# Turning a step's carried-over block behind the step's first head products

## The chip, the cores and the metric

The kernel runs on one core of a Trainium2 chip. The metric is the device time of one execution in microseconds (us), less being better; a change is compared with the kernel before by the median of several runs. Engines work side by side, each through its own instructions in order, and wait for one another by semaphores: PE (TensorE, matrix products), ACT (ScalarE), DVE (VectorE), POOL (GpSimd) and SP (it issues the loads).

## What is computed

Two models run one after the other on 8 sequences of 100 rows of 512 numbers, with a context of 8 x 361 x 512: a single-head cross-attention, then a block with two 16-head cross-attentions and an MLP.

```python
def _cross_attention(q_in, kv_in, wq, bq, wk, bk, wv, bv, wo, bo, bias_k, bias_v):
    qh = (q_in @ wq + bq).reshape(b, q_len, H, K)          # H = 16 heads of K = 128
    kh = concatenate([kv_in @ wk + bk, bias_k])            # 361 + 1 rows
    vh = concatenate([kv_in @ wv + bv, bias_v])
    weights = softmax(einsum('bqhk,bthk->bhqt', qh, kh) / sqrt(K))
    ctx = einsum('bhqt,bthk->bqhk', weights, vh)
    return ctx @ wo + bo

def _forward(x, xf_1, xf_2, ...):
    x = x + _cross_attention(layer_norm(x), xf_1, ...1)
    x = x + _cross_attention(layer_norm(x), xf_2, ...2)
    h = layer_norm(x)
    return x + gelu(h @ w_fc1 + b_fc1) @ w_fc2 + b_fc2
```

## The kernel before

The batch is worked on in two halves of 4 sequences. Each half has two attention layers and the MLP, so there are four **passes** through `layer` (`ph` 0 to 3 in the code, passes 1 to 4 here). Every number is held as two parts, `hi` and `lo`, and every product is three matmuls (`mm3`): hi by hi, lo by hi, hi by lo (lines 608 to 610). So whatever PE leaves in PSUM is first rounded to a `hi` by ACT, and then DVE takes the rest as `lo`; only then can PE read it.

The keys are never formed. A head's query goes through the head's key weights back to the 512 columns of the input ("through keys"), and is scored against the context itself. The 16 heads by 100 rows of a sequence are 1600 rows, cut into 13 blocks of 125 (the last 100). `UNITS` joins the blocks into six units of two blocks (the last of three), and `STEPS` is the list of (unit k, sequence b), 24 steps a pass.

What a step does to a block: **scores** (12 matmuls of 362 columns), the maximum (`maxima` on DVE, a copy and a reduction), the exponential (`exps` on ACT, with a read of the sum), the division (`normalise` on DVE, a reciprocal and a multiplication of `prob`), the **turning** (`turn_probs` on PE, three transposes of `prob` into one PSUM bank, `PT_BANK`), its two parts (`probs_hi` on ACT writes `pT_hi`, `probs_lo` on DVE writes `pT_lo`), and, when both blocks of a unit are turned, `attend` on PE: 36 matmuls of weights by context rows.

The blocks are turned one after the other in their order, and the last block of a step is turned in the next step: the *carried-over* block. `attend` of a step runs in the next step too, and waits for `pt_lo`, which DVE gives with that block's `probs_lo`. Step (2, 3), say, does on PE: scores of its block 0, turning of the block carried over from (2, 2), head products, scores of its block 1, `attend` of (2, 2), turning of its own block 0.

**Head products** fill in between. `PIECES` names, for a place of a step, which products of which head run there: `q` (a head's query, 12 matmuls, one output), `k` (through keys, 12 matmuls, four outputs), `v` (values, 13 matmuls, one output), `o` (projection, 12 matmuls, four outputs, which DVE adds to `xT`). Place "a" lies between the two scores, place "b" at the step's end. Ordinary steps with something in place "a" are, in each pass, these twelve:

- one `k`: (0,1), (0,2), (2,2), (2,3), (4,2), (4,3)
- one `v`: (1,1), (3,1)
- `q` and `o`: (1,2), (3,2)
- `o` and `k`: (1,3), (3,3)

The first two steps of units 2 and 4 (`LATE`) have an order of their own in other branches.

The outputs of head products and of `attend` go round five PSUM banks (`MBUFS`, `free_bank`): an output waits until DVE is through with the one five before it. The weights of head products come by SP through `stage`, and POOL splits them into `wbuf_hi` (line 490) and `wbuf_lo` (line 540), four buffers on; a split waits until PE has used the weights four before. In the first pass there is one thing more: DVE makes ten sums over late key weights (`late_key_sums`, line 1397), each of which waits for a load that is issued behind the sum before.

Every engine runs its list in the order that is written out by hand: for PE, ACT and DVE the loop over `STEPS` at lines 936 to 975, 1265 to 1304 and 1676 to 1725.

Of the kernel before, what the change touches and what calls it, by code (L numbers as in the profile page):

```python
# [68 lines left out]
def pieces(place):  # L69
    return [(word[0], int(word[1:])) for word in PIECES.get(place, "").split()]  # L70
# [61 lines left out]
def build(nc, xT_d, ctxT_d, ctx_d, l0w_d, alpha_d, head_w_d, cols_d, rows_d, norm_d, mlp_w_d, mlp_b_d, out_d):  # L132
# [3 lines left out]
    with ExitStack() as ctx:  # L136
# [468 lines left out]
        def _(pe):  # L605
# [194 lines left out]
            def layer(half, l):  # L800
# [79 lines left out]
                def run_pieces(place, start=0):  # L880
                    for kind, h in pieces(place)[start:]:
                        {"q": queries, "k": through_keys, "v": values, "o": project}[kind](h)

                def scores(k, b, x):
                    i = S_AT[k, b, x]
                    f0, rows = BLOCKS[UNITS[k][x]]
                    last_head = (f0 + rows - 1) // L
                    wait(pe, s_exp, ph * S_LAYER + i - 1)
                    ctx_b = slice(b * T, (b + 1) * T)
                    for c in range(DC):  # L890
                        pe.wait_ge(y_done, ph * R_LAYER + R_AT["k", last_head] + c + 1)
                        mm = mm3(bank[S_BANK + i % 2][0:rows, 0:T], a_hi[:, c, b, ring(f0, rows)],
                                 a_lo[:, c, b, ring(f0, rows)], c_hi[:, c, ctx_b], c_lo[:, c, ctx_b],
                                 start=(c == 0), stop=(c == DC - 1))
                    mm.then_inc(s_mm, 1)
# [38 lines left out]
                before = None  # L934
                for k, b in STEPS:
                    last = None if before is None else (*before, len(UNITS[before[0]]) - 1)
                    if k in LATE and b == 0:
                        scores(k, b, 0)
                        turn_probs(*last)
                        scores(k, b + 1, 0)  # L940
                        attend(*before)
                        turn_probs(k, b, 0)
                        run_pieces((k, b, "b"))
                        scores(k, b, 1)
                    elif k in LATE and b == 1:
                        run_pieces((k, b, "a"))
                        scores(k, b, 1)
                        turn_probs(*last)
                        run_pieces((k, b, "m"))
                        attend(*before)  # L950
                        turn_probs(k, b, 0)
                        run_pieces((k, b, "b"))
                    else:
                        scores(k, b, 0)
                        if before is not None:
                            turn_probs(*last)
                        run_pieces((k, b, "a"))
                        scores(k, b, 1)
                        if before is not None:
                            attend(*before)  # L960
                        turn_probs(k, b, 0)
                        run_pieces((k, b, "b"))
                        if len(UNITS[k]) == 3 and b == 0:
                            turn_probs(k, b, 1)
                            scores(k, b, 2)
                        elif len(UNITS[k]) == 3:
                            scores(k, b, 2)
                            turn_probs(k, b, 1)
                    before = k, b
# [55 lines left out]
        def _(act):  # L1025
# [146 lines left out]
            def layer(half, l):  # L1172
# [44 lines left out]
                def run_pieces(place, start=0):  # L1217
                    for kind, h in pieces(place)[start:]:
                        if kind != "o":
                            {"q": queries_hi, "k": through_keys_hi, "v": values_hi}[kind](h)  # L1220
# [44 lines left out]
                before = None  # L1265
                for k, b in STEPS:
                    last = None if before is None else (*before, len(UNITS[before[0]]) - 1)
                    if k in LATE and b == 0:
                        probs_hi(*last)
                        exps(k, b, 0)  # L1270
                        exps(k, b + 1, 0)
                        first_rows_hi(*before)
                        attended_hi(*before)
                        probs_hi(k, b, 0)
                        run_pieces((k, b, "b"))
                        exps(k, b, 1)
                    elif k in LATE and b == 1:
                        run_pieces((k, b, "a"))
                        probs_hi(*last)
                        run_pieces((k, b, "m"))  # L1280
                        first_rows_hi(*before)
                        attended_hi(*before)
                        probs_hi(k, b, 0)
                        exps(k, b, 1)
                        run_pieces((k, b, "b"))
                    else:
                        if before is not None:
                            probs_hi(*last)
                        exps(k, b, 0)
                        run_pieces((k, b, "a"))  # L1290
                        if before is not None:
                            first_rows_hi(*before)
                        exps(k, b, 1)
                        if before is not None:
                            attended_hi(*before)
                        probs_hi(k, b, 0)
                        run_pieces((k, b, "b"))
                        if len(UNITS[k]) == 3:
                            probs_hi(k, b, 1)
                            exps(k, b, 2)  # L1300
                    before = k, b
# [64 lines left out]
        def _(dve):  # L1366
# [211 lines left out]
            def layer(half, l):  # L1578
# [95 lines left out]
                for k, b in STEPS:  # L1674
                    last = None if before is None else (*before, len(UNITS[before[0]]) - 1)
                    if k in LATE and b == 0:
                        maxima(k, b, 0)
                        probs_lo(*last)
                        normalise(k, b, 0)
                        maxima(k, b + 1, 0)  # L1680
                        normalise(k, b + 1, 0)
                        first_rows_lo(*before)
                        attended_lo(*before)
                        probs_lo(k, b, 0)
                        run_pieces((k, b, "b"))
                        maxima(k, b, 1)
                        normalise(k, b, 1)
                    elif k in LATE and b == 1:
                        run_pieces((k, b, "a"))
                        maxima(k, b, 1)  # L1690
                        probs_lo(*last)
                        run_pieces((k, b, "m"))
                        first_rows_lo(*before)
                        attended_lo(*before)
                        probs_lo(k, b, 0)
                        normalise(k, b, 1)
                        run_pieces((k, b, "b"))
                    else:
                        maxima(k, b, 0)
                        if before is not None:  # L1700
                            probs_lo(*last)
                        normalise(k, b, 0)
                        run_pieces((k, b, "a"))
                        if ph == 0 and "a" in LATE_KEYS_AT.get((k, b), ""):
                            late_key_sums(next(keys))
                        maxima(k, b, 1)
                        if before is not None:
                            first_rows_lo(*before)
                        normalise(k, b, 1)
                        if before is not None:  # L1710
                            attended_lo(*before)
                        probs_lo(k, b, 0)
                        run_pieces((k, b, "b"))
                        if len(UNITS[k]) == 3 and b == 0:
                            probs_lo(k, b, 1)
                            maxima(k, b, 2)
                            normalise(k, b, 2)
                        elif len(UNITS[k]) == 3:
                            maxima(k, b, 2)
                            probs_lo(k, b, 1)  # L1720
                            normalise(k, b, 2)
                    if ph == 0 and "b" in LATE_KEYS_AT.get((k, b), ""):
                        late_key_sums(next(keys))
                    if ph == 0 and (k, b) == (3, 2):
                        key_parts(1)
                    before = k, b
# [114 lines left out]
```

## Time and profile before

| | |
|---|---|
| runs before, median (lowest to highest of 3) | 1829.16 us (1825.69 to 6293.97) |
| profiled execution, device time | 1830.22 us |
| its span (first to last instruction) | 1828.4 us |
| PE busy | 1801.8 us, 99% |
| DVE, ACT, POOL busy | 1125.2, 804.9, 761.4 us |
| mean granted TensorE clock | 0.999 |

The profile is of one execution. A line of the timeline gives start and duration in us from the span's start, the engine, the line of the program, what is written and read, how many instructions are joined, and in brackets how long the engine sat idle before and what ended that.

### The profile page before, as it was taken

How to read it: one execution, taken by the hardware profiler on the slowest of the kernel's cores; microseconds unless marked ns; L12 is line 12 of the kernel's file. 1: busy time of each engine (PE TensorE's matmuls, PEld its weight loads, DVE VectorE, ACT ScalarE, POOL GpSimd, SP SyncE). 2: the span in 40 equal slices, each digit the busy share in tenths (PEclk: the TensorE clock that was granted, in tenths of full speed). 3: DMA queues.
4: the chain of work that ended last, by engine and by line, in shares of the span. 5: the costliest groups of instructions: out<-in, count | busy, mean ns of one | idle time of the engine just before them, and what ended most of it. 6: DMA issues, size and time to landing. Idle time of an engine off the chain costs nothing.

```text
span 1828.4 us, 30720 instructions
## 1 busy us (share of the span) xinstructions
PE 1801.8 (99%) x11524; PEld 1768.3 (97%) x11524; DVE 1125.2 (62%) x2588; ACT 804.9 (44%) x1868; POOL 761.4 (42%) x624
## 2 busy tenths in 40 slices
PE   8989999999999999999999999999999999999999
PEld 5889999999999999999999999999999999999999
DVE  3667656565575565556687655556566556555565
ACT  3634334434344443344475443444435434434354
POOL 2674252352351453531478245252255252352344
PEclk9999999999999999999999999999999999999999
DMA  8833221111120121210373011111022021121132
GB/s 254 241 111 94 62 64 30 47 60 34 33 69 23 41 64 36 59 40 13 127 218 94 30 47 59 35 53 41 24 58 60 24 64 30 47 59 35 46 98 84
DMA packets 73590, 123.80 MB, mean 68 GB/s; under 512 B 13888, under 2 KB 25536, under 8 KB 73444
## 3 DMA queue, kind: packets, MB, share of 16 engines
q1 hardware_dynamic: 71140, 117.64, 22.0%
q10 hardware_dynamic: 2304, 4.20, 0.7%
q8 instruction: 94, 1.54, 0.4%
q14 instruction: 52, 0.43, 0.1%
HBM read 119.20 MB, written 2.61 MB: 67 GB/s over the span
## 4 chain that ended last, share of the span: by engine, by line
PE 88%; DVE 5%; DMA 4%; ACT 1%; SPq 1%; issue 1%; POOL 0%; DVEq 0%; ACTq 0%
PE psum L608 27%; PE psum L609 27%; PE psum L610 27%; PE psum L906 4%; DMA ctxT_in<-ctxT_dram 1%; DMA ctx_rows_in<-ctx_dram 1%; DMA key_stage_late<-head_w_dram 1%; PE psum L779 1%; PE psum L870 1%; PE psum L621 1%; DVE xT L1576 1%; PE psum L617 1%; DVE psum L1544 1%; PE psum L618 0%; PE psum L797 0%
## 5 line engine op out<-in xcount | busy, mean ns | idle before, releaser
L490 POOL TENSOR_TENSOR wbuf_hi<-stage,zero_col 128x512 fp32r<-128x512 f32 x256 | 267.9, 1047 | 917.8 <-PE psum L610 605.1
L540 POOL TENSOR_TENSOR wbuf_lo<-stage,wbuf_hi 128x512 fp32r<-128x512 f32 x256 | 330.2, 1290 | 20.0
L610 PE MATMUL psum<-pT_hi,ctx_rows_lo 121*128 121x250 f32 (+3 forms) x1152 | 332.2, 288 | 0.0
L608 PE MATMUL psum<-pT_hi,ctx_rows_hi 121*128 121x250 f32 (+3 forms) x1152 | 331.6, 288 | 0.0
L609 PE MATMUL psum<-pT_lo,ctx_rows_hi 121*128 121x250 f32 (+3 forms) x1152 | 331.1, 287 | 0.0
L608 PE MATMUL psum<-ctxT_hi,a_hi 128*125 128x362 f32 (+1 forms) x832 | 280.4, 337 | 0.0
L610 PE MATMUL psum<-ctxT_hi,a_lo 128*125 128x362 f32 (+1 forms) x832 | 273.1, 328 | 0.0
L609 PE MATMUL psum<-ctxT_lo,a_hi 128*125 128x362 f32 (+1 forms) x832 | 272.7, 328 | 0.0
L1371 DVE TENSOR_TENSOR a_lo<-psum,a_hi 128x500 fp32r<-128x500 f32 (+2 forms) x288 | 145.9, 526 | 195.1 <-ACT a_hi L1027 194.2
L608 PE MATMUL psum<-a_hi,wbuf_hi 128*128 128x400 f32 x720 | 253.1, 352 | 0.0
L609 PE MATMUL psum<-a_lo,wbuf_hi 128*128 128x400 f32 x720 | 247.8, 344 | 0.0
L610 PE MATMUL psum<-a_hi,wbuf_lo 128*128 128x400 f32 x720 | 247.8, 344 | 0.0
L1027 ACT ACTIVATE a_hi<-psum 128x500 fp32r<-128x500 f32 (+2 forms) x288 | 127.6, 467 | 218.7 <-PE psum L610 217.8
L609 PEld LDWEIGHTS psum<-pT_lo,ctx_rows_hi 121*128 121x128 f32 (+1 forms) x1152 | 219.3, 190 | 0.0
L608 PEld LDWEIGHTS psum<-pT_hi,ctx_rows_hi 121*128 121x128 f32 (+1 forms) x1152 | 218.5, 190 | 0.1
L610 PEld LDWEIGHTS psum<-pT_hi,ctx_rows_lo 121*128 121x128 f32 (+1 forms) x1152 | 217.7, 189 | 0.0
L1231 ACT ACTIVATE prob<-psum,stats 125x362 f32<-125x362 f32 (+1 forms) x208 | 117.3, 564 | 183.1 <-DVE stats L1633 183.1
L1027 ACT ACTIVATE pT_hi<-psum 121x375 fp32r<-121x375 f32 (+1 forms) x208 | 99.9, 480 | 202.8 <-PE psum L906 202.8
L1375 DVE SCALAR_TENSOR_TENSOR a_lo<-psum,cols,a_hi 128x400 fp32r<-128x400 f32 x116 | 73.5, 633 | 175.2 <-ACT a_hi L1214 108.6
L1576 DVE TENSOR_TENSOR xT<-psum,xT 128x400 f32<-128x400 f32 x352 | 176.6, 564 | 0.1
L609 PEld LDWEIGHTS psum<-ctxT_lo,a_hi 128*125 128x125 f32 (+1 forms) x832 | 153.5, 184 | 0.1
L608 PEld LDWEIGHTS psum<-ctxT_hi,a_hi 128*125 128x125 f32 (+1 forms) x832 | 153.3, 184 | 0.1
(185 smaller groups left out, 3549.7 us busy)
## 6 DMA issues: line engine op xcount, KB each, us to landing
stage<-head_w_dram SPq DMA_DIRECT2D x256, 256.0 KB, 2.6
mlp_stage<-mlp_w_dram SPq DMA_DIRECT2D x32, 512.0 KB, 4.2
ctx_rows_in<-ctx_dram SPq DMA_DIRECT2D x12, 726.0 KB
ctxT_in<-ctxT_dram SPq DMA_DIRECT2D x12, 724.0 KB, 11.0
key_stage<-head_w_dram SPq DMA_DIRECT2D x22, 256.0 KB, 8.7
l0w<-l_w_dram ACTq DMA_DIRECT2D x16, 256.0 KB, 9.1
key_stage_late<-head_w_dram SPq DMA_DIRECT2D x10, 256.0 KB, 3.5
out_dram<-y_out SPq DMA_DIRECT2D x8, 200.0 KB, 2.7
```

The costliest lines, as they stand in the source:

```text
L490: return nc.gpsimd.tensor_tensor(out, in_, zero_col[0:in_.shape[0], :].broadcast_to(tuple(in_.shape)), ALU.add)
L540: nc.gpsimd.tensor_tensor(lo, held, hi.bitcast(F32), ALU.subtract).then_inc(stage_free, 1)
L608: pe.matmul(out, a_h, x_hi, start=start, stop=False)
L609: pe.matmul(out, a_h, x_lo, start=False, stop=False)
L610: return pe.matmul(out, a_l, x_hi, start=False, stop=stop)
L617: pe.matmul(out, a_h(c), h_hi[:, c, piece(n)], start=(c == 0), stop=False)
L906: mm = pe.transpose(bank[PT_BANK][0:t_rows, t * PT_STEP:t * PT_STEP + rows], prob[0:rows, i % 2, t0:t0 + t_rows], ident[0:rows, 0:rows])
L1027: return nc.scalar.activation(out, in_, ACT.Copy)
L1231: nc.scalar.activation(prob[0:rows, i % 2, :], bank[S_BANK + i % 2][0:rows, 0:T], ACT.Exp, bias=st[:, 0:1], accum_out=st[:, 2:3]).then_inc ...
L1371: return nc.vector.tensor_tensor(out, value, hi.bitcast(F32), sub)
L1375: return nc.vector.scalar_tensor_tensor(out=out, in0=value, scalar=bias, in1=hi.bitcast(F32), op0=ALU.add, op1=sub)
L1576: return nc.vector.tensor_tensor(out, value, x, ALU.add)
```

## The change

In ordinary steps that have something in place "a", the carried-over block is turned behind those products and no longer ahead of them. `probs_hi` on ACT and `probs_lo` on DVE of this block move the same way, behind the parts that these engines make of the products. Steps with nothing in place "a" keep their order. That is 12 steps a pass and 48 in all. No instruction is added or taken away.

```diff
@@ PE
                         scores(k, b, 0)
+                        run_pieces((k, b, "a"))
                         if before is not None:
                             turn_probs(*last)
-                        run_pieces((k, b, "a"))
                         scores(k, b, 1)
@@ ACT
-                        if before is not None:
+                        if before is not None and not pieces((k, b, "a")):
                             probs_hi(*last)
                         exps(k, b, 0)
                         run_pieces((k, b, "a"))
+                        if before is not None and pieces((k, b, "a")):
+                            probs_hi(*last)
                         if before is not None:
                             first_rows_hi(*before)
@@ DVE
                         maxima(k, b, 0)
-                        if before is not None:
+                        if before is not None and not pieces((k, b, "a")):
                             probs_lo(*last)
                         normalise(k, b, 0)
                         run_pieces((k, b, "a"))
+                        if before is not None and pieces((k, b, "a")):
+                            probs_lo(*last)
                         if ph == 0 and "a" in LATE_KEYS_AT.get((k, b), ""):
```

On PE, in step (0, 1), before: the end of the scores of block 0 (`ctxT`, `a_hi`), the three transposes of `prob`, and the first matmuls of k3.

```order
L608 MATMUL psum<-ctxT_hi,a_hi 125x362
L609 MATMUL psum<-ctxT_lo,a_hi 125x362
L610 MATMUL psum<-ctxT_hi,a_lo 125x362
L906 MATMUL psum<-ident,prob 121x125 x2
L906 MATMUL psum<-ident,prob 120x125
L608 MATMUL psum<-a_hi,wbuf3_hi 128x400
L609 MATMUL psum<-a_lo,wbuf3_hi 128x400
```

On PE at the same place now, the last matmuls of k3, the transposes, and the first scores of block 1.

```order
L608 MATMUL psum<-a_hi,wbuf3_hi 128x400
L609 MATMUL psum<-a_lo,wbuf3_hi 128x400
L610 MATMUL psum<-a_hi,wbuf3_lo 128x400
L906 MATMUL psum<-ident,prob 121x125 x2
L906 MATMUL psum<-ident,prob 120x125
L608 MATMUL psum<-ctxT_hi,a_hi 125x362
L609 MATMUL psum<-ctxT_lo,a_hi 125x362
L610 MATMUL psum<-ctxT_hi,a_lo 125x362
```

The transposes have moved by the 12 matmuls of k3, from between scores and k3 to between k3 and scores.

On DVE, in step (2, 3) of the first pass, before: `maxima` of block 0 (copy and reduction), `pT_lo` of the carried-over block, `normalise` of block 0, the four `a_lo` of k9, `maxima` of block 1.

```order
L1631 COPY psum<-s0_cols 125x1
L1633 TENSOR_REDUCE stats<-psum 125x1
L1371 TENSOR_TENSOR pT_lo<-psum,pT_hi 121x3x125
L1640 RECIPROCAL stats<-stats 125x1
L1642 TENSOR_SCALAR prob<-prob,stats 125x362
L1380 SCALAR_TENSOR_TENSOR a_lo<-psum,a_hi 128x4x100 x4
L1631 COPY psum<-s0_cols 125x1
```

On DVE in the same step now (the lines of this part of the file stand two further down).

```order
L1633 COPY psum<-s0_cols 125x1
L1635 TENSOR_REDUCE stats<-psum 125x1
L1642 RECIPROCAL stats<-stats 125x1
L1644 TENSOR_SCALAR prob<-prob,stats 125x362
L1382 SCALAR_TENSOR_TENSOR a_lo<-psum,a_hi 128x4x100 x4
L1373 TENSOR_TENSOR pT_lo<-psum,pT_hi 121x3x125
L1633 COPY psum<-s0_cols 125x1
```

`pT_lo` stood third and is now sixth, behind `normalise` and all four `a_lo`.

## Rows read from the trace of the kernel before

**Rows 1.** The page: busy time of each engine, the chain that ended last.
```profile
PE 1801.8 (99%) x11524; PEld 1768.3 (97%) x11524; DVE 1125.2 (62%) x2588; ACT 804.9 (44%) x1868; POOL 761.4 (42%) x624
PE 88%; DVE 5%; DMA 4%; ACT 1%; SPq 1%; issue 1%; POOL 0%; DVEq 0%; ACTq 0%
```

**Rows 2.** Waits of PE: who waited, for whom, total us, times, longest.
```profile
PE psum L906 <- DVE pT_lo L1371: 4.8, 6, 1.2
```

**Rows 3.** Timeline, PE, step (2,3) of pass 1.
```profile
293.83 0.48 PE L906 MATMUL psum<-ident,prob 125*121 125x125 f32 x3
294.07 0.43 PE L608 MATMUL psum<-a_hi,wbuf_hi 128*128 128x400 f32 x1
...
296.15 0.34 PE L610 MATMUL psum<-a_hi,wbuf_lo 128*128 128x400 f32 x1
296.33 0.33 PE L608 MATMUL psum<-ctxT_hi,a_hi 128*125 128x362 f32 x1
...
298.32 0.28 PE L608 MATMUL psum<-pT_hi,ctx_rows_hi 121*128 121x250 f32 x1
```

**Rows 4.** Timeline, DVE, the same step.
```profile
294.22 0.53 DVE L1633 TENSOR_REDUCE stats<-psum 125x1 f32<-125x362 f32 x1
294.87 0.55 DVE L1371 TENSOR_TENSOR pT_lo<-psum,pT_hi 121x375 fp32r<-121x375 f32 x1
295.68 0.41 DVE L1642 TENSOR_SCALAR prob<-prob,stats 125x362 f32<-125x362 f32 x1
296.00 2.01 DVE L1380 SCALAR_TENSOR_TENSOR a_lo<-psum,a_hi 128x400 fp32r<-128x400 f32 x4
```

**Rows 5.** Timeline, ACT, the same step.
```profile
294.35 0.49 ACT L1027 ACTIVATE pT_hi<-psum 121x375 fp32r<-121x375 f32 x1 [1.73 <-PE psum L906]
295.34 1.69 ACT L1210 ACTIVATE a_hi<-psum 128x400 fp32r<-128x400 f32 x4
```

**Rows 6.** Timeline, PE and DVE, step (0,1) of pass 2.
```profile
541.86 0.55 PE L906 MATMUL psum<-ident,prob 125*121 125x125 f32 x3 [1.19 <-DVE pT_lo L1371]
546.45 0.28 PE L608 MATMUL psum<-pT_hi,ctx_rows_hi 121*128 121x250 f32 x1
541.18 0.53 DVE L1371 TENSOR_TENSOR pT_lo<-psum,pT_hi 121x375 fp32r<-121x375 f32 x1
541.82 0.53 DVE L1633 TENSOR_REDUCE stats<-psum 125x1 f32<-125x362 f32 x1
543.71 0.41 DVE L1642 TENSOR_SCALAR prob<-prob,stats 125x362 f32<-125x362 f32 x1
```

**Rows 7.** Timeline, POOL: steps (2,3) of pass 1 and (0,1) of pass 2.
```profile
296.64 1.04 POOL L490 TENSOR_TENSOR wbuf_hi<-stage,zero_col 128x512 fp32r<-128x512 f32 x1 [2.10 <-PE psum L610]
544.76 1.04 POOL L490 TENSOR_TENSOR wbuf_hi<-stage,zero_col 128x512 fp32r<-128x512 f32 x1 [3.71 <-PE psum L610]
```

**Rows 8.** Timeline, DVE and POOL, step (0,2) of pass 1; then PE.
```profile
170.87 1.09 DVE L1642 TENSOR_SCALAR prob<-prob,stats 125x362 f32<-125x362 f32 x1
171.88 2.00 DVE L1380 SCALAR_TENSOR_TENSOR a_lo<-psum,a_hi 128x400 fp32r<-128x400 f32 x4
170.71 1.04 POOL L490 TENSOR_TENSOR wbuf_hi<-stage,zero_col 128x512 fp32r<-128x512 f32 x1 [1.99 <-PE psum L610]
172.39 0.28 PE L608 MATMUL psum<-pT_hi,ctx_rows_hi 121*128 121x250 f32 x1
198.14 0.55 PE L906 MATMUL psum<-ident,prob 125*121 125x125 f32 x3 [0.60 <-DVE pT_lo L1371]
```

**Rows 9.** Timeline, DVE and PE, step (1,2) of pass 1.
```profile
216.35 2.25 DVE L1575 SCALAR_TENSOR_TENSOR xT<-psum,norm_p,xT 128x400 f32<-128x400 f32 x4
218.47 0.28 PE L608 MATMUL psum<-pT_hi,ctx_rows_hi 121*128 121x250 f32 x1
```

**Rows 10.** Timeline, DVE and PE, step (1,3) of pass 1.
```profile
231.56 2.01 DVE L1576 TENSOR_TENSOR xT<-psum,xT 128x400 f32<-128x400 f32 x4
232.44 0.35 PE L608 MATMUL psum<-a_hi,wbuf_hi 128*128 128x400 f32 x1
```

## The prediction

> **What bounds the kernel now.** I read the page first. PE is busy for 1801.8 us, 99% of the span, and 88% of the chain that ended last is PE [rows 1]. So the time is the sum of what PE issues plus what PE waits, and a change that adds and removes nothing on PE can act on the waits alone. The waits of PE come next: at the transposes of the attention layers (line 906) it waits for pT_lo, 4.8 us in 6 places [rows 2]. That is about the most that a later turning could win. The timeline of an ordinary step, third, shows that PE has no wait at all there: scores, transposes, products, scores and attend follow one another, with the twelve product matmuls in 296.33-294.07 = 2.26 us and the twelve of the scores in 298.32-296.33 = 1.99, 0.17 each [rows 3].
>
> So the question is what becomes late. The timelines of DVE and ACT answer it [rows 4, 5]. Before, pT_lo of the carried-over block starts at 294.87 and ends at 295.42, and attend, which needs it, starts at 298.32 [rows 3, 4]: 2.9 us to spare. The change spends these 2.9 us.
>
> **The change, part by part.**
>
> *What PE issues* is the same list with 48 groups of three transposes moved. The order scores, turn, head, scores becomes scores, head, turn, scores. The one visible cost of a turn, a first product matmul of 0.43 instead of 0.34 us behind it [rows 3], leaves 0.18 for each of the others (2.26-0.09 = 2.17 over twelve), and it then falls on the first scores matmul instead. I take 0 for this.
>
> *One k product, step (2,3).* Count from 293.83, where the scores end. On PE k9 now runs there, the turning at about 296.08, the scores of block 1 from 296.33, and attend would start at 298.32 as before. On ACT pT_hi moves behind four a_hi, which end at 297.03 [rows 5], or near it; the turning gives pT_hi 0.52 us later (293.83 to 294.35), at 296.6, so ACT's own queue decides and pT_hi is there at about 297.4. On DVE the maximum ends at 294.75, and the exponential is set by it, not by pT_hi: the multiplication stays at 295.68 and the four a_lo at 296.00 to 298.01 [rows 4]. They follow each other at (2.01-0.56)/3 = 0.48 us, so pT_lo starts at 296.00+4x0.48 = 297.93, and ends 0.55 later at 298.48. From the end of pT_lo to a PE that waits for it there are 541.86-(541.18+0.53) = 0.15 us [rows 6]. Attend starts at 298.63 and not at 298.32: 0.30 late. Behind a wait PE's next matmuls are slow to come too: three transposes take 0.55 us there against 0.48 [rows 3, 6], so 0.07 more. **0.37 us a step.** The six k steps of a pass are 24 in all. (0,1) is counted apart, as is (0,2) of pass 1; the other 19 are the same work on the same queues. 19 x 0.37 = **+7.0 us**. Bounds: from nothing, if DVE takes pT_lo sooner, to 0.5 us a step.
>
> *o and k, steps (1,3) and (3,3), 8 in all.* DVE has eight jobs of 0.48 us from 231.56 [rows 10], and pT_lo behind them is done at 231.56+8x0.48+0.55 = 235.95. Attend is due (24 product matmuls and not 12) at 232.44+9x0.18+1.99 = 236.1: just in time. But PE starts its products 0.24 us earlier (293.83 and not 294.07 [rows 3]), and without the 0.09, while DVE does not: the second output of k needs the bank of the first output of o, which DVE frees at 231.56+0.57 = 232.13, plus 0.15 makes 232.28. PE was there at 232.44 [rows 10] and is now there at 232.11. It waits 0.15, and 0.07 behind the wait. 8 x 0.2 = **+1.7 us**.
>
> *v, and q with o, 16 steps.* With q and o, DVE has five jobs and not the eight of o and k, under the same 24 matmuls of PE, so it is done sooner than the case above, which was just in time. A v is one job and not four; it waits for PE's last product matmul, and its two parts end about 1.6 us behind that (an estimate, from 296.15 to 298.01 in a k step [rows 3, 4], which has a little queue in it), 3.9 us behind the scores and 0.3 before the k step's 4.18 (298.01-293.83). **0** for all, but in pass 1 (below); upper bound 0.1 each.
>
> *Step (0,1), 4 in all.* Here PE waits today. In pass 2 the turning stands 1.19 us for pT_lo of the block before [rows 6], since nothing lies between. The change puts k3 into this hole: the last scores matmul ends at 541.86-1.19 = 540.67, so k3 can start at 540.51 and its last matmul at 540.51+11x0.18 = 542.5. But attend then waits for the chain on DVE: the maximum ends at 542.35, and the exponential, which stands behind pT_hi today and with it behind the waiting turning, can follow at once, 0.44 us sooner (an estimate: the step from 542.35 to 543.71 is 1.36 us, and in step (2,3), where nothing is in the way, it is 295.68-294.75 = 0.93). So the multiplication could start at 543.27 instead of 543.71, four a_lo and pT_lo behind it. That alone would bring attend to 546.2 instead of 546.45. There is a catch on POOL. It splits the next weights 0.49 us behind the start of a k product's last matmul (296.15 [rows 3] to 296.64 [rows 7]), now at 543.0 instead of 544.76 [rows 7], and for 1.04 us. A multiplication of prob that meets such a split lasts until 0.2 us behind its end: 170.87 plus 1.09 is 171.96, the split ran from 170.71 to 171.75 [rows 8]. So it ends at 544.25 instead of 544.12, pT_lo follows, and attend starts at about 546.75, 0.3 later than today. The same holds in pass 4; in passes 1 and 3 the wait today is shorter and POOL is already in its second half, line 540, which by the same reckoning ends sooner: 0.1 us won. Sum **+0.4 us**, bounds -1 (no meeting) to +1.2. On this the Trainium skill ("SBUF — State Buffer", "SBUF: two separate sides") says that VectorE and GpSimd share a port pair as an exclusive lock, and that the one that starts first holds it for its whole instruction. By that rule, the trace agrees for this multiplication (1.09 us in a meeting, 0.41 without). Without the rule the step would be a gain of 0.2.
>
> *Pass 1, with its late key sums.* In (0,2) attend is due at 172.39 but the four a_lo end at 173.88 [rows 8]; pT_lo behind them makes it 2 us late. Most of this is given back: in the steps behind, DVE and through it PE wait for key loads anyway (0.60 us at 198.14 [rows 8], and another of the six places just before), and in (1,1) v0 no longer stands behind that waiting turning. In (1,2) the four xT end at 218.60 and attend was due at 218.47 [rows 9]: with pT_lo 0.6 to 0.75 late. I take **+0.7 us** for the pass, bounds 0 to 2.5.
>
> Sum 7.0+1.7+0.4+0.7 = **9.8 us**. The profiled execution took 1830.2, so 1840.0 on its own scale; the median shown is 1 us lower, so I predict **1839.0 us**, 0.5% slower.
>
> **The rivals.**
>
> *A: pT_lo is in time everywhere.* The lateness in the k steps is 0.3 us behind 4.5 us of work, so a small error in DVE's pace hides it. Against: DVE's order is fixed and 297.93+0.55 is plain adding. Without the 7.0 and the 1.7 it would give 1830.
>
> *B, faster: the holes are filled and nothing takes their place.* Four (0,1) steps and the one at 198.14 are five of the six places with 4.8 us [rows 2]. If attend did not come to wait, 1829.2-4.8 = 1824.4, 0.3% faster. It decides if DVE would make pT_lo ahead of the a_lo, which the order forbids.
>
> *C, over 2% slower: the split meets the multiplication in every k and o-k step.* Now POOL's split starts at the last k matmul plus 0.49: 293.83+2.0+0.49 = 296.3, and the multiplication starts at 295.68 [rows 4]. If it came 0.65 us later, it would end with the split at 297.55 and not at 296.09, 1.46 us a step; 27 steps make 39 us on top, 1878. Nothing in the profile makes it later.
>
> *D: the waits are deeper but below 2%.* A late attend delays turning and DVE jobs that I hold to be free; another 0.3 us in each of 48 steps gives 1853.
>
> **How the numbers follow.** My forecast 0.70, A 0.13, B 0.05, C 0.02, D 0.10. The range 1830 to 1848 takes in my forecast with the bounds above, A in most, and the lower half of D; it leaves out B, C and the rest. A measurement of this kernel tells about 2% (36.6 us) from no change; of the cases C alone reaches it, so faster 0.01, same 0.96, slower 0.03.
>
> **What would show it.** In the waits of PE a new row: attend (line 608, reading ctx_rows) waiting for pT_lo some 20 to 27 times, near 0.2 to 0.3 us each (the view counts less than the delay, since it starts at the end of the matmul before). The waits of the transposes for pT_lo sink from 4.8 us to under 1. In step (2,3) pT_lo stands at about 4.1 us behind the scores' end. In (1,3) a product waits for xT. PE's busy time stays near 1802. I am wrong if attend does not wait in the k steps, or if the multiplication lasts over 0.41 us in more than a few of them.

## The result and the profile after

The changed kernel took 1839.17 us in the median (9 runs, 1833.73 to 1842.26), the kernel before 1829.16 us (9 runs; one of them took 6293.97 us, which does not move the median). The ratio is 1.0052, with a 95% interval of 1.0038 to 1.0067: 0.5% slower, and so far inside the 2% that count as no change. The forecast was 1839.0 us.

The page of the changed kernel: span and instructions, busy time of each engine, the shares of the chain that ended last.

```profile
span 1837.9 us, 30720 instructions
...
PE 1809.7 (98%) x11524; PEld 1767.7 (96%) x11524; DVE 1122.6 (61%) x2588; ACT 809.0 (44%) x1868; POOL 760.3 (41%) x624
...
PE 89%; DVE 6%; ACT 2%; issue 1%; DMA 1%; POOL 0%; SPq 0%; DVEq 0%; ACTq 0%
```

The span is 9.5 us longer than the 1828.4 of before. The instructions are the same, yet PE's busy time went from 1801.8 [rows 1] to 1809.7. The waits of PE (total us, times, longest) do not show where it went:

```profile
PE psum L608 <- DVE pT_lo L1373: 6.5, 6, 1.6
PE psum L642 <- DMA l0w<-l_w_dram: 5.1, 1, 5.1
```

The transposes of the layers wait for pT_lo no more (before 4.8 us in 6 places [rows 2]), and attend waits in 6 places: the four (0,1), and (0,2) and (1,2) of pass 1. The wait for `l0w` is not new (5.2 us before). An ordinary k step is not among these. Here is the one that the prediction followed, (2,3) of pass 1, first PE and then DVE and ACT, in the timeline (start, duration, engine, line):

```profile
294.74 0.33 PE L610 MATMUL psum<-ctxT_hi,a_lo 128*125 128x362 f32 x1
294.90 0.35 PE L608 MATMUL psum<-a_hi,wbuf_hi 128*128 128x400 f32 x1
...
297.09 0.48 PE L906 MATMUL psum<-ident,prob 125*121 125x125 f32 x3
297.34 0.41 PE L608 MATMUL psum<-ctxT_hi,a_hi 128*125 128x362 f32 x1
...
299.25 0.33 PE L610 MATMUL psum<-ctxT_hi,a_lo 128*125 128x362 f32 x1
299.60 0.39 PE L608 MATMUL psum<-pT_hi,ctx_rows_hi 121*128 121x250 f32 x1
299.82 0.28 PE L609 MATMUL psum<-pT_lo,ctx_rows_hi 121*128 121x250 f32 x1
```

```profile
296.75 0.41 DVE L1644 TENSOR_SCALAR prob<-prob,stats 125x362 f32<-125x362 f32 x1
297.08 2.01 DVE L1382 SCALAR_TENSOR_TENSOR a_lo<-psum,a_hi 128x400 fp32r<-128x400 f32 x4
299.00 0.54 DVE L1373 TENSOR_TENSOR pT_lo<-psum,pT_hi 121x375 fp32r<-121x375 f32 x1
...
297.96 0.52 ACT L1027 ACTIVATE pT_hi<-psum 121x375 fp32r<-121x375 f32 x1
```

The scores end at 294.90, where k9 starts. pT_lo starts 4.10 us behind that, as forecast, and ends at 299.54. ACT had its pT_hi ready at 298.48, 0.52 before DVE took it up, so pT_lo waited for DVE's own queue. Attend is due 0.17 behind the last scores matmul, at 299.42, and starts at 299.60: 0.18 late. Its second matmul follows after 0.22 and not 0.12 (before, one stood 0.12 behind the other), 0.10 more. With 0.03 that the due time itself moved (4.52 behind the scores' end, before 298.32-293.83 = 4.49 [rows 3]) this makes 0.31 us. The view of the waits has nothing of it, because it counts from the end of the matmul before: that one is given as 299.25 to 299.58, so only 0.02 of idle time is left. What is lost shows in the distances from start to start, and in the higher "busy" time of PE.

So I compared the two traces by starts: for each step the start of PE's turning of the step's own block 0, after less before, and of that the growth from step to step. The growth, summed over like steps, in us:

| steps | forecast | measured |
|---|---|---|
| 19 ordinary k steps | +7.0 | +6.0 (0.29 to 0.36 each) |
| 8 steps of o and k | +1.7 | +1.1 (0.13 to 0.15 each) |
| 14 of v, and of q with o, beyond the first steps of pass 1 | 0 | -0.1 |
| (0,1), passes 1, 2, 3, 4 | -0.1, +0.3, -0.1, +0.3 | -0.5, +0.4, +1.1, +0.4 |
| pass 1, (0,2) to (1,2) | +0.7 | +1.2 |
| before the layers, and the rest | 0 | 0.0 |
| all | 9.8 | 9.5 (the rounded terms above give 9.6) |

### The profile page after: what moved, and what is told of

Read it like the earlier page. It is cut to its first block, busy times and chain, and to the rows that moved or that the text cites. A ratio compares the mean times of both kernels' runs of the same rounds, so it can differ in the third digit from the quotient of the medians.

```text
span 1837.9 us, 30720 instructions
## 1 busy us (share of the span) xinstructions
PE 1809.7 (98%) x11524; PEld 1767.7 (96%) x11524; DVE 1122.6 (61%) x2588; ACT 809.0 (44%) x1868; POOL 760.3 (41%) x624
## 4 chain that ended last, share of the span: by engine, by line
PE 89%; DVE 6%; ACT 2%; issue 1%; DMA 1%; POOL 0%; SPq 0%; DVEq 0%; ACTq 0%
PE psum L608 27%; PE psum L610 27%; PE psum L609 27%; PE psum L906 3%; PE psum L642 2%; DMA key_stage_late<-head_w_dram 1%; DVE a_lo L1382 1%; PE psum L779 1%; PE psum L870 1%; PE psum L621 1%; DVE xT L1578 1%; PE psum L617 1%; DVE stats L1635 1%; DVE psum L1546 1%; DVE prob L1644 0%
## 5 line engine op out<-in xcount | busy, mean ns | idle before, releaser
L608 PE MATMUL psum<-ctxT_hi,a_hi 128*125 128x362 f32 (+1 forms) x832 | 284.3, 342 | 0.0
```

Of the source, the lines that this page charges most:

```text
L608: pe.matmul(out, a_h, x_hi, start=start, stop=False)
```

## The experiments

All are compared in the same way. The last column but one is a step in which something happened that the change has no part in (the last section). "Before the layers" is the part up to the first turning, where PE waits for loads; it was between 5.9 us shorter and 0.9 longer than in the profiled execution of before, in kernels that are the same up to there. So one execution's span says little here, and its steps say more. "Rest" goes up to the last turning; the 0.63 of e4 lies at the start of pass 3 and was not followed. The kernels e2, e3, e5, e6, e8 and e8b ran once each, so of these only the steps are compared.

| kernel | before the layers | k (19) | o, k (7) | v; q, o (14) | (0,1) (4) | pass 1, (0,2)-(1,2) | (3,3), pass 1 | rest |
|---|---|---|---|---|---|---|---|---|
| the change | -0.05 | +6.04 | +0.91 | -0.09 | +1.27 | +1.23 | +0.15 | 0.02 |
| e1_k_only | -5.86 | +5.93 | 0.00 | 0.00 | -0.90 | +1.21 | +0.53 | 0.00 |
| e2_v_qo_only | -0.44 | +0.01 | 0.00 | -0.09 | -0.19 | -0.02 | +0.55 | -0.06 |
| e3_ok_only | -3.71 | +0.02 | +0.96 | 0.00 | -0.28 | -0.07 | +1.59 | -0.08 |
| e4_pe_alone | -3.32 | -0.02 | 0.00 | +10.92 | -4.55 | +1.85 | 0.00 | +0.63 |
| e5_k_dve_first | -3.62 | -0.02 | 0.00 | 0.00 | -3.20 | +1.08 | +0.56 | +0.04 |
| e6_k_dve_more | -2.41 | +15.13 | +0.09 | -0.23 | +3.33 | +3.53 | +0.55 | +0.10 |
| e7_first_steps | -1.56 | +0.01 | 0.00 | 0.00 | -3.89 | -0.52 | +0.55 | +0.05 |
| e8_pool_held | -2.00 | +6.03 | +0.96 | -0.09 | -3.01 | +1.36 | +1.63 | -0.02 |
| e8b_change_again | -2.08 | +6.05 | +1.00 | -0.10 | +1.40 | +1.25 | +1.61 | +0.05 |
| e9_pe_alone_k_v | +0.92 | -0.02 | 0.00 | -0.05 | -4.55 | +0.25 | 0.00 | -0.05 |

### The change in one kind of step

Three kernels make the change in some steps only, on all engines, and keep the order of before in the others:

```diff
+def behind(k, b):
+    kinds = "".join(kind for kind, _ in pieces((k, b, "a")))
+    return kinds == "k"     # e2: kinds in ("v", "qo"); e3: kinds == "ok"
@@ PE (ACT and DVE alike)
                         scores(k, b, 0)
+                        if before is not None and not behind(k, b):
+                            turn_probs(*last)
                         run_pieces((k, b, "a"))
-                        if before is not None:
+                        if before is not None and behind(k, b):
                             turn_probs(*last)
```

> Only the 24 steps with one k product turn the carried-over block behind it, on all three engines; the v, q-o and o-k steps keep the order of before. Theory 1 (pT_lo stands behind the product's low parts on DVE, so attend waits): almost all of the change's 9.5 us of span stays, +8 to +9, since the k steps hold 0.32 us each and the four (0,1) steps about 1.3 together. Rival (every moved turning costs PE the same, whatever stands on DVE): 24/48 of it, +4.8.

> Only the 16 steps with v, or with q and o, are changed. Theory 1: DVE has little in front of pT_lo there, span 0 in passes 2 to 4; in pass 1 at most 0.7 us lost in (1,2) and some 0.5 won at (1,1), since v0 no longer stands behind a waiting turning. Rival of equal cost: +3.2.

> Only the 8 steps with o and k are changed. Theory 1: +0.13 us each, +1.0 in all, and it is a product matmul that waits for DVE's xT of four outputs before, not attend. Rival of equal cost: +1.6.

The k steps alone took 1836.81 us (ratio 1.0029, 1.0015 to 1.0043), and in them 5.93 us of the change's 6.04 came back, the same 0.3 in each. The steps of v, and of q with o, cost nothing (1829.97 in one run). The steps of o and k cost 0.13 to 0.17 each (1828.65 in one run, with 3.7 us less before the layers). So in these three groups the price sits in the steps where the prediction put it, and the parts add up.

The (0,1) steps do not add up. They are k steps, so e1 changes them as the change does, and yet they gave -0.90 us in e1 and +1.27 in the change. The 2.2 us between them are most of what e1 (6.5 us over before in the median) fell short of the 8 to 9 that were expected of it. The section on the first step of a pass comes back to this.

### Which queue makes attend late

In e5 everything is as in e1, but DVE takes pT_lo behind the multiplication and ahead of the a_lo; ACT's order stays. If ACT's pT_hi were late, nothing would be gained.

```diff
@@ DVE, against e1
                         normalise(k, b, 0)
-                        run_pieces((k, b, "a"))
                         if before is not None and behind(k, b):
                             probs_lo(*last)
+                        run_pieces((k, b, "a"))
```

> As the run with k steps alone, but DVE takes pT_lo ahead of the product's four a_lo (behind normalise); PE and ACT keep the changed order, with pT_hi behind four a_hi. Theory 1 (DVE's queue makes attend late): pT_lo is done 4.2 us behind the scores, attend is due at 4.5 and no longer waits in ordinary k steps; the (0,1) steps win about 1 us each; span 1825 to 1828. Theory 2 (ACT's queue, pT_hi behind four a_hi, makes it late): attend stays 0.3 late, span +8 as with k steps alone.

In e6, DVE does one job more between the a_lo and pT_lo, a maximum over `xT` into a column that nothing reads; the results do not depend on it.

```diff
@@ DVE, against e1
                         if before is not None and behind(k, b):
+                            nc.vector.tensor_reduce(spare[:, :], xT[:, 0, :], AX_X, ALU.max)
                             probs_lo(*last)
```

> As the run with k steps alone, with one more job on DVE in those 24 steps, a maximum over 400 columns of xT that nobody reads (about 0.5 us), between the product's a_lo and pT_lo. Theory 1: attend is later by all of it in every one of the 24 steps, about +0.4 to +0.5 us each, +10 to +12 us on top of the k steps alone, less some 1 in pass 1. Theory 2 (ACT's queue): nothing on top, or the little by which DVE becomes the later one.

e5 brought the 19 k steps to -0.02 us in all, from +5.93. Step (2,3) of pass 1, DVE and PE:

```profile
293.90 0.55 DVE L1380 TENSOR_TENSOR pT_lo<-psum,pT_hi 121x375 fp32r<-121x375 f32 x1 [1.34 <-ACT pT_hi L1034]
294.37 2.01 DVE L1389 SCALAR_TENSOR_TENSOR a_lo<-psum,a_hi 128x400 fp32r<-128x400 f32 x4
...
294.64 0.33 PE L615 MATMUL psum<-ctxT_hi,a_lo 128*125 128x362 f32 x1
294.81 0.28 PE L613 MATMUL psum<-pT_hi,ctx_rows_hi 121*128 121x250 f32 x1
```

Attend follows the scores at 0.17. DVE even stands 1.34 us for pT_hi before, and that delays the a_lo, whose next reader is far enough away. In e6 the same row stands behind the job that was put in, and now the lateness is long enough for the bracket to show it:

```profile
299.91 0.56 DVE L1715 TENSOR_REDUCE spare<-xT 128x1 f32<-128x400 f32 x1
300.39 0.54 DVE L1381 TENSOR_TENSOR pT_lo<-psum,pT_hi 121x375 fp32r<-121x375 f32 x1
...
300.98 0.39 PE L614 MATMUL psum<-pT_hi,ctx_rows_hi 121*128 121x250 f32 x1 [0.51 <-DVE pT_lo L1381]
```

The job moves pT_lo by 0.48 us, and the 19 steps went from 5.93 to 15.13 us, by 9.20/19 = 0.48 each. So an ordinary k step pays one for one what stands ahead of pT_lo in DVE's queue, and nothing once the a_lo stand behind it. The expectation had put e6 at 10 to 12 us over e1; the k steps gave 9.2, and the (0,1) steps another 4.2 that were not followed. The waits of PE have the row that the prediction had looked for after the change, in as many places as there are k steps:

```profile
PE psum L614 <- DVE pT_lo L1381: 17.1, 24, 2.0
```

### PE alone

What if only PE turns later, and ACT and DVE keep the order of before? Then their next jobs in line wait for PE.

```diff
+    return kinds in ("k", "v", "qo")        # e9: kinds in ("k", "v")
@@ PE as in e1; ACT and DVE as before the change
```

> PE alone turns the carried-over block behind the products, in the k, v and q-o steps; ACT and DVE keep the order of before, with pT_hi and pT_lo ahead of the product's parts (the o-k steps stay as before, since there DVE would have to free a bank first). Theory 1: pT_lo is ready 3.9 us behind the scores and attend is due at 4.5, so no attend waits; the waiting turnings of the (0,1) steps are filled by k3 and nothing takes their place: -3 to -4 us in passes 2 to 4 and at most +1 in pass 1, where the key sums move back, together a span of 1825 to 1827. Rival (the turning costs PE by its new place alone): 1833 or more.

> PE alone turns behind the products, in the k and v steps only; q-o steps are as before. In the run with q-o too, each of these 8 steps was 1.57 us longer, since the second half of attend needs the bank of q's output, whose low part then stands behind a turning that comes late. If that is all that was wrong there, the 12.5 us go and the 4.3 us won in the (0,1) and (1,1) steps stay: about -4 us, 1826 for a median of 1830. If turning late on PE has another cost, the k steps show it (0.0 there is expected).

The expectation of e4 was wrong: 1837.66 us, ratio 1.0041 (1.0029 to 1.0053). The k steps cost nothing, and (0,1) gained 4.6 us. But each of the eight steps of q and o lost 1.57, 12.6 us in all. The waits of PE name the reason, in exactly 8 places, and the timeline of (1,2) in pass 2 shows it on DVE, POOL and PE:

```profile
PE psum L613 <- DVE a_lo L1382: 10.7, 8, 1.3
```

```profile
600.51 0.55 DVE L1378 TENSOR_TENSOR pT_lo<-psum,pT_hi 121x375 fp32r<-121x375 f32 x1 [4.46 <-ACT pT_hi L1034]
601.05 0.16 DVE L1647 RECIPROCAL stats<-stats 125x1 f32<-125x1 f32 x1
601.25 1.33 DVE L1649 TENSOR_SCALAR prob<-prob,stats 125x362 f32<-125x362 f32 x1
602.51 0.62 DVE L1382 SCALAR_TENSOR_TENSOR a_lo<-psum,cols,a_hi 128x400 fp32r<-128x400 f32 x1
...
601.10 1.28 POOL L545 TENSOR_TENSOR wbuf_lo<-stage,wbuf_hi 128x512 fp32r<-128x512 f32 x1
...
603.27 0.36 PE L613 MATMUL psum<-pT_hi,ctx_rows_hi 121*128 121x250 f32 x1 [1.34 <-DVE a_lo L1382]
```

q and o are 24 matmuls and five banks. DVE stands 4.46 us for the turning behind them, and q's a_lo waits in line. Attend's first matmul writes to the bank that this a_lo frees, so it is PE that pays: the bank, not pT_lo, is what attend waits for. The delayed multiplication also meets POOL's split, in all eight of these steps: 1.33 us and not 0.41. DVE has no gap between it and q's a_lo, and ACT's a_hi was there at 601.51, so by these rows some 0.9 of the 1.57 us is the meeting's (an estimate; it was not tried apart).

e9 is the test of that: PE alone in the steps of k and v, q with o left as before. It took 1826.53 us, ratio 0.9988 (0.9978 to 0.9999), and the q and o steps were back at 0. So it is those steps that made e4 slow. Against the 1829.11 beside it e9 won 2.6 us in the median where about 4 were expected; by the steps it won 4.3, with the part before the layers 0.9 longer. The first matmul of attend is the one that waits in e4, not the second half that the expectation names.

### The first step of a pass, and POOL

The prediction put +0.4 on (0,1) and it was +1.3. The largest part is pass 3, DVE and POOL in the changed kernel:

```profile
1012.49 1.41 DVE L1644 TENSOR_SCALAR prob<-prob,stats 125x362 f32<-125x362 f32 x1
...
1011.28 1.04 POOL L490 TENSOR_TENSOR wbuf_hi<-stage,zero_col 128x512 fp32r<-128x512 f32 x1 [1.01 <-DMA stage<-head_w_dram]
1012.40 1.29 POOL L540 TENSOR_TENSOR wbuf_lo<-stage,wbuf_hi 128x512 fp32r<-128x512 f32 x1
```

The multiplication starts 0.09 us behind the start of the second half of a split and lasts until 1013.90, 0.21 behind its end. To see what the meeting costs, e8 keeps the change and lets POOL wait with three splits for the multiplication of (0,1):

```diff
@@ POOL
+                        if WBUFS + W_AT["k", 3] - 2 <= i <= WBUFS + W_AT["k", 3]:
+                            pool.wait_ge(s_norm, ph * S_LAYER + S_AT[0, 1, 0] + 1)
                         split_weights(ph, i)
```

> The changed kernel, with POOL held before the splits of k4, v0 and v1 until step (0,1)'s multiplication of prob is done, so that none of them can meet it. If meetings with POOL's splits set how late attend is in the (0,1) steps (+0.35, +1.10 and +0.36 us in passes 2 to 4 of the profiled execution, against the turning's wait of before), the multiplication takes 0.41 us in all four, and these steps come out 0.2 to 0.9 us shorter than in the changed kernel: -0.2 in passes 2 and 4, about -0.2 in pass 3 where today's wait is shorter. If something else on DVE sets it, they stay at +0.35 and more. The ordinary k steps keep their 0.32 us.

> The changed kernel once more, to see what differs from one execution to the next: ordinary k steps +0.28 to +0.34 us and o-k steps +0.13 again, each to 0.02; the (0,1) steps, which hang on when the weight loads land, and the part before the layers may differ by a microsecond or more.

Side by side, e8 took 1835.07 us and the change again 1839.39. The (0,1) steps were -3.01 in e8 and +1.40 in e8b, 4.4 us or 1.1 a step, more than the 0.2 to 0.9 that were expected; the other groups of steps agree within about 0.1. (e8b also shows how well the change repeats: the steps that it touches, without (3,3) of pass 1, sum to 9.6 us, and to 9.4 in the first execution. That one step gave +1.61 and not +0.15.) Here is (0,1) of pass 2 in the change and in e8, DVE's multiplication and the split:

```profile
545.47 0.96 DVE L1644 TENSOR_SCALAR prob<-prob,stats 125x362 f32<-125x362 f32 x1
...
545.19 1.04 POOL L490 TENSOR_TENSOR wbuf_hi<-stage,zero_col 128x512 fp32r<-128x512 f32 x1 [1.93 <-PE psum L610]
...
548.87 0.38 PE L608 MATMUL psum<-pT_hi,ctx_rows_hi 121*128 121x250 f32 x1 [1.52 <-DVE pT_lo L1373]
```

```profile
544.28 0.41 DVE L1646 TENSOR_SCALAR prob<-prob,stats 125x362 f32<-125x362 f32 x1
...
544.77 1.04 POOL L490 TENSOR_TENSOR wbuf_hi<-stage,zero_col 128x512 fp32r<-128x512 f32 x1 [5.84 <-DVE prob L1646]
```

More came back than this one meeting (0.96-0.41 = 0.55), because e8 holds an earlier split too: the multiplication of (0,0)'s second block, ahead in DVE's line, lasted 1.26 us in the change and 0.41 in e8. That earlier meeting stood in the kernel before as well (1.22 us), so e8 also wins what the change did not lose.

These two durations account for the (0,1) steps. Take the growth in e8, where both are 0.41, and add what the two lasted beyond that: in all twelve (0,1) steps of the change, of e8b and of e1 the sum is the measured growth, to 0.03 us. In pass 2 the change had 1.26 and 0.96, and -1.05+0.85+0.55 = +0.35 was measured; e1, with the same order in this step, had 0.41 and 0.47, and gave -0.99. So whether (0,1) wins or loses hangs on where POOL's splits fall, and that differs from one execution to the next.

The Trainium skill ("SBUF — State Buffer", "SBUF: two separate sides") says that VectorE and GpSimd share a pair of ports as an exclusive lock, which the one that starts first keeps for its whole instruction. The trace agrees: the multiplication takes 0.41 us where no split is running, and where one is it never ends before the split does (245 meetings in the twelve traces).

### A kernel faster than both

> The order of before but for six steps: in (0,1) of passes 2 to 4 PE alone turns behind k3 (ACT and DVE as before), and in (0,1) and (1,1) of pass 1 all three engines do as in the change. Theory 1: the waiting turnings of 0.5 to 1.3 us are filled and no attend waits: about -1.4, -0.7 and -1.4 us in passes 2 to 4 and -0.5 to -1 in pass 1, together -4 to -4.5 us, a span near 1824. Rival: the wait moves to another place of the same chain on DVE (the next attend or turning), and the span stays at 1828.

```diff
+def all_behind(ph, k, b):
+    return ph == 0 and (k, b) in ((0, 1), (1, 1))
+def turn_behind(ph, k, b):
+    return (k, b) == (0, 1) or all_behind(ph, k, b)
@@ PE turns behind the products where turn_behind, ACT and DVE where all_behind
```

The order of before stays everywhere but in steps that can gain: in (0,1) of passes 2 to 4 PE alone turns later, and in (0,1) and (1,1) of pass 1 all three engines do. 1824.67 us against 1830.95, ratio 0.9966 (0.9955 to 0.9978). The (0,1) steps gave 3.9 us (-0.3, -1.4, -0.8, -1.4) and pass 1 another 0.5. The rest of the 6 us in the medians lies in no step of the trace but in the part before the layers, or in what single executions vary by.

## Why the prediction came out

**What bounds the kernel: right.** The change adds nothing to PE's list, and the 9.5 us are PE coming late to the same matmuls.

**The k step: the mechanism right, both of its sizes a little off.** pT_lo stood at 4.10 us behind the scores (forecast 297.93-293.83 = 4.10), and e5 and e6 showed that it is DVE's queue that decides. The step "attend starts at 298.63, 0.30 late" was 0.18 plus 0.03 of a later due time. The 0.15 us from the end of pT_lo to PE was taken from a transpose [rows 6]; attend starts 299.60-299.54 = 0.06 behind it, and in (0,1) of pass 2 as well (548.28+0.53 = 548.81, then 548.87). What follows the wait cost 0.10 and not 0.07. So 0.32 a step and not 0.37, 6.0 us and not 7.0.

**o and k: right in kind, too large.** The second output of k meets DVE at the bank, as said. In (1,3) of pass 1 two products that should stand 0.18 apart stand 0.28 apart:

```profile
232.56 0.35 PE L610 MATMUL psum<-a_hi,wbuf_lo 128*128 128x400 f32 x1
232.84 0.45 PE L608 MATMUL psum<-a_hi,wbuf_hi 128*128 128x400 f32 x1
```

That is 0.10 late where 0.15 was forecast, and the step cost 0.13 and not 0.2. e3 gave the same by itself.

**v, and q with o: right.** Moved on all three engines it is free (e2). Moved on PE alone it costs 1.57 a step with q and o (e4). The argument had counted DVE's jobs but not what happens to q's bank when DVE stands for the turning instead; the change as made does not do that.

**(0,1): right in passes 2 and 4, wrong in 1 and 3.** +0.3 was forecast for each of passes 2 and 4, and +0.35 and +0.36 measured, in e8b as well. The catch is real, and so is its size: without its own meeting (0.55) pass 2 would stand at -0.20, as the prediction said. But e1 gave -0.99 in the same step of pass 2, because both splits fell elsewhere: that they met here is in part luck. The step that failed is "in passes 1 and 3 POOL is already in its second half, which ends sooner: 0.1 us won". In pass 3 POOL was in its second half, but at its start, so the multiplication lay under nearly all of its 1.29 us: +1.1. In pass 1 it met only the last 0.25 of the split (0.46 us), and the step won 0.5. In e8b the two gave +0.85 and -0.16. One start on the trace of before does not tell which side of a split a job will land on once both have moved. With POOL out of the way the four steps gave 3.0 us, where the prediction's bound for "no meeting" was 1: it had counted only the meeting in (0,1), and not the one of the block ahead in DVE's line, which costs in the kernel before too.

**Pass 1: right in sign.** (0,2) lost 1.8 us (forecast about 2), (1,0) and (1,1) won 0.9, and (1,2) lost 0.4 (forecast 0.6 to 0.75). Net 1.2 against 0.7: I had counted on more coming back. Only the 0.5 of (1,0) came back for the loss in (0,2); the 0.4 of (1,1) is a gain of its own, since e2 and e7 have it with (0,2) as before.

The errors cancel: 1.0 and 0.6 too much in the k and the o-k steps, 0.9 and 0.5 too little in (0,1) and pass 1. 0.2 us between forecast and median is luck to that extent; the sum by its terms was good to about 1 us each.

**The rivals.** A (in time everywhere) falls with the 6.0 us in the k steps. B (faster) needs pT_lo ahead of the a_lo, and e5 is that kernel: its steps were 1.5 us below before, not the 4.8 of the waits. What B describes, the holes filled and nothing in their place, is e7: 4.4 us in the steps. C (the split meets the multiplication in every k step) did not happen in the change. In e4 and e9 it did, in all 19 ordinary k steps, and they stayed at -0.02 us in all: there pT_lo stands ahead of the multiplication, so that price, too, hangs on the order in DVE's queue. In the q-o steps of e4 it cost. D (deeper waits) falls as well: no ordinary step lost over 0.36.

**What would show it.** The transposes' waits sank to nothing for pT_lo, and a product in (1,3) came late, both as said. Two signs were wrong. Attend should have waited in 20 to 27 places of the waits, and the view has 6; PE's busy time should have stayed near 1802, and was 1809.7. The prediction's own remark, that the view counts from the end of the matmul before, was not carried through: that end lies 0.33 behind its start, a lateness of 0.18 behind a pitch of 0.17 leaves 0.02, and the loss shows as busy time.

## What to carry to other kernels

A later job on the bounding engine is free only if each of the engines that hand on its result has it early enough in its own line; so count, for every queue, what now stands ahead of it, and put it ahead of work that nobody waits for soon (e5). Turn the order only in the steps that have a hole (e7), not in all that look alike. And look for losses of a few tenths of a microsecond in the distances of starts: the waits do not show them, and the busy time shows only that the same instructions took longer. Last, a price that hangs on where another engine's job falls is a draw: compare such a step over several executions before calling it won or lost.

## What the runs showed of the hardware

When VectorE and GpSimd start within 10 ns of each other, either can go first. In pass 1, ahead of step (3,3), DVE's subtraction of a part of the key weights (64 elements a partition, two inputs from SBUF) comes at the same moment as the second half of a split. Before, DVE and POOL:

```profile
344.52 0.22 DVE L1371 TENSOR_TENSOR w_lo<-w,w_hi 128x64 fp32r<-128x64 f32 x1
...
344.52 1.37 POOL L540 TENSOR_TENSOR wbuf_lo<-stage,wbuf_hi 128x512 fp32r<-128x512 f32 x1
```

In the change run again (e8b), and the product that came late through it:

```profile
344.33 1.37 DVE L1373 TENSOR_TENSOR w_lo<-w,w_hi 128x64 fp32r<-128x64 f32 x1
...
344.32 1.29 POOL L540 TENSOR_TENSOR wbuf_lo<-stage,wbuf_hi 128x512 fp32r<-128x512 f32 x1
...
348.95 0.45 PE L608 MATMUL psum<-a_hi,wbuf_hi 128*128 128x400 f32 x1 [1.38 <-DVE xT L1578]
```

If DVE goes first, POOL loses 0.08 us (1.37 and not 1.29). If POOL does, DVE waits the split out and loses 1.15 (1.37 and not 0.22). By the trace's nanoseconds POOL started first in all twelve executions: by 4 to 6 ns in the four in which DVE still went first, by 6 to 9 ns in the eight in which POOL did. So the rule of the first start does not settle it this close. The same program gave +0.15 us in this step in one profiled execution and +1.61 in the other. Kernels without the change in this step gave 0.00 where DVE went first and about +0.55 where POOL did. That is up to 1.5 us of luck in one execution, and it has nothing to do with an edit.

The other surprise is how much a multiplication under a split costs beyond the split: it ended 0.20 or 0.21 us behind the split's end in all of the meetings shown here (in pass 3 of the change, 1012.49+1.41 = 1013.90 against 1012.40+1.29 = 1013.69; in (0,1) of pass 2, 545.47+0.96 = 546.43 against 545.19+1.04 = 546.23, 0.20). Of the 245 meetings in the twelve traces 199 ended 0.20 or 0.21 behind the split, the others 0.22 to 0.36.
